# A first message pass that gathers normalized features instead of rows of a precomputed table

## The chip, the cores and the metric

One program runs on one core of a Trainium2 chip. The metric is the device time of one execution in microseconds (us), and the time of a version is the median of its runs. Besides the runs, one execution was recorded by the hardware profiler; all rows shown here are from it. The engines are PE (TensorE: matmul; PEld is its weight load), DVE (VectorE), ACT (ScalarE), POOL (GpSimd) and SP (SyncE, here only an issuer of DMAs).

## The reference, cut to what matters

A graph of 3125 nodes with 128 features and 53125 directed edges, sorted by destination, goes through four layers, each added to the input and normalized:

```python
# layer 0: four dense-looking steps over the same graph
for l in range(4):
    agg = segment_sum(x[src], dst);  h = relu((x + agg) @ W1[l] + b1[l]);  x = h @ W2[l] + b2[l]
# layer 1, 8 kinds of edges: a mean over each kind, the kernel's "first pass"
out = x @ root + bias
for r in range(8):
    s = segment_sum((x @ W[r])[src] * (edge_type_8 == r), dst)
    c = segment_sum(edge_type_8 == r, dst)
    out = out + s / maximum(c, 1)
out = relu(out)
# layer 2, 16 kinds: alpha[kind] * (x @ w_rel[kind])[src] summed at dst, plus indegree * (x @ update), relu
# layer 3, 8 kinds: gate * (x @ W[kind] + bias)[src] summed at dst, plus x @ loop_weight, relu
```

Between the layers stands `y = layernorm(previous input + layer output)`.

## The kernel before, in words

The 3125 nodes are 25 blocks of 128, the edges 416 tiles of 128. The program has these stages.

1. **Setup and adjacency** (0 to 300 us): PE builds the dense adjacency matrix `adj` in SBUF from one-hot products.
2. **Layer 0** (300 to 735 us): four dense multiplications with `adj`, `block_sums` (L1052), first the four early chunks of 512 nodes, then the three late ones; ACT applies the relu (L1330), PE multiplies by the next matrix (`layer_rows`, L987) and DVE adds the bias into `un` (L1683). After the last layer the space of `adj` is reused for everything that follows, so loads and the first norm wait for its last product.
3. **First table** (735 to 806 us): five sets of five blocks are normalized on DVE (`norm`, L1716 to L1736), turned by PE (L1126) and multiplied by the eight kind matrices and the root matrix (L1135). ACT and DVE copy the products out of PSUM (L1357, L1759) and SP writes 512 KB a block to `table1` (L665): row `8 * node + kind` holds `x @ W[kind]`. POOL copies the normalized features into `xn`.
4. **Edge weights** (803 to 866 us, DVE, `edge_weights`): for each edge one over the number of edges of its kind at its destination, `w1`.
5. **Three passes** (806 to 2466 us) of the same form. POOL issues one indirect DMA per tile of 128 edges (`gathers`, L808), which brings 128 rows of 512 bytes into `ring`, a ring of 51 tiles (three turns of 17). ACT scales each tile by its edge weights (`take`, L1384). PE multiplies a one-hot of 128 destinations by the tile (`sums`, L1199) and so adds it to the sum of a block in PSUM; where a tile straddles two blocks it is multiplied twice, so a turn of 17 tiles has 18 steps in three groups of six. DVE makes the one-hots (`hot_group`, L1590), adds and normalizes a finished block (`block_sum`, `block_norm`, L1798 to L1817), PE turns it (`transposed`, L1152) and multiplies it for the next table (`products`, L1165), ACT and DVE copy that out (L1406, L1827), and SP writes it (L691). One turn carries the tiles of about one block. A slot of the ring is handed on to POOL by ACT (`hand_on`, L1367) once the group that used it is done. A pass starts to gather when the table before it is written whole.

Every engine has its own fixed order of work and waits on semaphores; nothing is scheduled at run time. In the second and third pass the loop over turns is the same; the second has 16 kinds, the third gates.

## Time and profile before

| | us |
|---|---|
| median of 3 runs (lowest, highest) | 2472.38 (2465.28, 2472.53) |
| the profiled execution | 2467.42 |
| its span, first to last instruction | 2465.6 |
| POOL busy, indirect gathers x1248 | 1347.4, 1216.7 |
| PE busy, mean granted clock | 1431.8, 0.754 |
| DVE busy | 923.6 |
| ACT busy | 633.1 |

Busy time of a group is summed over the whole span, so an engine can be busy half of the time and still set the end of each stage, and of an indirect gather the profile counts only the part in which POOL works: from one to the next there are 0.30 us more of issue. PE's clock is told as the granted share of full speed: 1.0 is 2.4 GHz and 0.5 is 1.2 GHz, and the number of a stretch is the mean of the two over it.

### The profile page before, as it was taken

Reading aid. Unit: us, or ns where it says so; the run is one execution under the profiler, and the core shown is the slowest. Engines: PE = TensorE matmul, PEld = TensorE weight load, DVE = VectorE, ACT = ScalarE, POOL = GpSimd, SP = SyncE. Lnnn points to the kernel's source line nnn. Section 1 sums busy time; section 2 is a strip of 40 time slices with the busy share of each in tenths; the row PEclk is TensorE's granted clock in tenths of the full one; section 3 lists DMA queues with packets and bytes.
Section 4 is the critical chain, followed back from the end, with each engine's and each line's share of the span. In section 5 each row is a group of like instructions: output and inputs, shape, how many; then the busy total and the mean of one; then the engine's idle time right before and its main releaser. Section 6 shows DMA issues by size and latency. Waiting matters only on the chain.

```text
span 2465.6 us, 30012 instructions
## 1 busy us (share of the span) xinstructions
PE 1431.8 (58%) x6376; PEld 929.6 (38%) x6481; DVE 923.6 (37%) x2317; ACT 633.1 (26%) x1671; POOL 1347.4 (55%) x1541
## 2 busy tenths in 40 slices
PE   5666599999999065555565255555454333333333
PEld 3333355455444044434343143334333233333333
DVE  6999622121116943333222453333333321222221
ACT  0677400000013043333333154444443100000000
POOL 1000015230221777777777477777777477777775
PEclk8888899999999577677766676767766666556665
DMA  0000001000026233333323222222222122222221
GB/s 20 0 0 0 18 14 11 7 5 0 5 40 246 56 89 106 106 105 106 105 87 106 83 69 78 77 78 78 76 70 77 60 55 56 55 55 56 56 55 47
DMA packets 120619, 148.87 MB, mean 60 GB/s; under 512 B 74779, under 2 KB 88737, under 8 KB 117362
## 3 DMA queue, kind: packets, MB, share of 16 engines
q0 software_dynamic: 40000, 81.89, 13.1%
q1 hardware_dynamic: 80562, 66.31, 8.2%
q8 instruction: 25, 0.41, 0.1%
q14 instruction: 32, 0.26, 0.0%
HBM read 91.39 MB, written 56.72 MB: 60 GB/s over the span
## 4 chain that ended last, share of the span: by engine, by line
POOL 45%; PE 26%; issue 17%; DVE 5%; ACT 4%; DMA 1%; SPq 1%; POOLq 1%; ACTq 0%; DVEq 0%
POOL adj L808 45%; PE acc L1052 16%; PE acc L943 4%; ACT adj L1305 2%; PE acc L1135 2%; ACT acc L1309 1%; PE acc L1199 1%; PE misc L987 1%; PE acc L1165 1%; DMA table<-adj 1%; DMA adj<-table,adj 1%; DVE adj L1937 0%; DVE adj L1908 0%; ACT adj L1384 0%; DVE adj L1910 0%
## 5 line engine op out<-in xcount | busy, mean ns | idle before, releaser
L808 POOL DMA_INDIRECT adj<-table,adj x1248 | 1216.7, 975 | 442.4 <-issue 378.4
L1199 PE MATMUL acc<-adj 128*128 x2640 | 524.9, 374 | 702.9 <-ACT adj L1384 321.8
L1199 PEld LDWEIGHTS acc<-adj 128*128 128x128 f32 x2640 | 473.0, 274 | 770.6 <-issue 770.2
L1384 ACT ACTIVATE adj<-adj 128x128 f32<-128x128 f32 x832 | 263.2, 390 | 573.5 <-DMA adj<-table,adj 489.3
L1052 PE MATMUL acc<-adj,feat 128*128 (+2 forms) x2042 | 399.7, 352 | 6.6 <-DVEq L1639 3.5
L758 POOL TENSOR_TENSOR node_rep<-node_rep,compb 128x128 f32<-128x128 f32 x128 | 57.2, 447 | 547.2 <-DMA node_rep<-in_L_gnn_weight_dram 538.4
L1590 DVE TENSOR_TENSOR adj<-acc,drel 128x768 f32<-128x768 f32 (+1 forms) x148 | 139.9, 948 | 453.7 <-PE acc L1199 453.2
L1052 PEld LDWEIGHTS acc<-adj,feat 128*128 (+1 forms) x2100 | 185.6, 98 | 212.0 <-DVEq L1639 3.4
L1165 PE MATMUL acc<-adj 128*128 128x512 f32 (+1 forms) x350 | 197.9, 711 | 71.5 <-ACT adj L1399 71.5
L943 PE MATMUL acc<-feat 128*128 128x400 bf16 x625 | 142.1, 387 | 76.6 <-ACT acc L1309 68.9
L1603 DVE TENSOR_SCALAR feat<-feat 128x400 bf16<-128x400 int16 x625 | 156.4, 318 | 0.0
L1367 ACT ACTIVATE adj<-feat 128x4 int32 (+1 forms) x196 | 33.7, 198 | 447.0 <-PE acc L1199 441.3
L1165 PEld LDWEIGHTS acc<-adj 128*128 128x128 f32 x350 | 83.2, 267 | 159.8 <-ACT adj L1399 84.3
L943 PEld LDWEIGHTS acc<-feat 128*128 128x128 bf16 x625 | 78.2, 126 | 141.0 <-issue 126.8
L1590 DVE TENSOR_TENSOR adj<-node_iob,drel 128x384 f32<-128x384 bf16 (+1 forms) x148 | 75.2, 551 | 147.7 <-PE acc L1199 147.7
L1330 ACT ACTIVATE feat<-acc,l0c 128x512 f32<-128x512 f32 (+1 forms) x28 | 15.6, 635 | 358.2 <-PE acc L1052 292.1
L1305 ACT ACTIVATE adj<-acc 128x800 f32 (+1 forms) x98 | 81.1, 827 | 54.8 <-PE acc L943 54.6
L1309 ACT ACTIVATE acc<-zerob 128x800 f32<-128x800 bf16 x98 | 82.5, 842 | 9.0
L1599 DVE TENSOR_TENSOR feat<-node_rep,temp 128x640 bf16<-128x640 bf16 x125 | 69.1, 553 | 21.4 <-PE acc L943 12.1
L1683 DVE TENSOR_TENSOR temp<-misc,l0c 128x512 f32<-128x512 f32 (+1 forms) x21 | 13.3, 633 | 144.9 <-PE misc L987 144.9
L1827 DVE COPY adj<-acc 128x512 f32<-128x512 f32 x25 | 17.3, 692 | 127.0 <-PE acc L1165 127.0
L1798 DVE TENSOR_TENSOR adj<-acc,adj 128x128 f32<-128x128 f32 x75 | 21.7, 289 | 103.2 <-PE acc L1199 103.0
(266 smaller groups left out, 1070.4 us busy)
## 6 DMA issues: line engine op xcount, KB each, us to landing
table<-adj SPq DMA_DIRECT2D x50, 512.0 KB, 2.8
table<-adj SPq DMA_DIRECT2D x25, 1024.0 KB, 4.2
adj<-table,adj POOLq DMA_INDIRECT x1250, 2.5
table<-adj SPq DMA_DIRECT2D x25, 64.0 KB, 1.8
temp<-in_x_dram SPq DMA_DIRECT2D x6, 256.0 KB, 3.1
out_dram<-adj SPq DMA_DIRECT2D x24, 64.0 KB, 1.6
wrel<-node_rep SPq DMA_DIRECT2D x16, 64.0 KB, 3.0
adj<-in_L_gnn_W_dram SPq DMA_DIRECT2D x2, 512.0 KB, 5.1
```

The costliest lines, as they stand in the source:

```text
L758: nc.gpsimd.tensor_tensor(sl_tmp if b else sl_out, of_b, by, ALU.mult).then_inc(slice_step, 1)
L808: pool.indirect_dma_start(ring[:, p_, 0:D], None, table, bass.IndirectOffsetOnAxis(ap=gidx[:, p_:p_ + 1], axis=0)).then_inc(msgs_in[u.r][c ...
L943: nc.tensor.matmul(acc[:, bass.ds(places[q * FG + j], FCOLS)], flo[:, q, :, j], foh[:, q, j, :], start=False, stop=True, skip_group_check= ...
L1052: last = nc.tensor.matmul(acc[:, c * KB:c * KB + chunk(c)], x3[:, s, bass.ds(b, 1), :].rearrange("p b f -> p (b f)"), adj[:, bass.ds(b, 1) ...
L1165: nc.tensor.matmul(o, xT1[:, b.r, :], table, start=True, stop=True).then_inc(prod_full[j], 1)
L1199: last = nc.tensor.matmul(acc[:, bass.ds(blk[s], width)], hot[:, c, j, :], ring_flat[:, bass.ds(place[s], width)], start=False, stop=True, ...
L1305: nc.scalar.activation(adj[:, :, bass.ds(i * (TURN * 2 * FB) + r * 2 * FB, 2 * FB)].rearrange("p h (k n) -> p h k n", k=2), fslots[r % FSL ...
L1309: nc.scalar.activation(fslots[r % FSLOTS], zerob[:, 0:FCOLS].unsqueeze(1).to_broadcast([P, 2, FCOLS]), ACT.Copy).then_inc(zeroed, 1)
L1384: last = nc.scalar.activation(o, o, ACT.Copy, scale=WEIGHT[ph][:, bass.ds(tiles_from(u, c) + j, 1)])
L1590: return nc.vector.tensor_tensor(o, numbers.unsqueeze(1).to_broadcast([P, n, P]), drel[:, bass.ds(s, n)].unsqueeze(2).to_broadcast([P, n, ...
L1599: nc.vector.tensor_tensor(flo[:, q, :, :], node_iof[:, :, :], flow[:, bass.ds(k * (FG * FNB) + q * FG, FG)].unsqueeze(1).to_broadcast([P, ...
L1603: last = nc.vector.tensor_scalar(foh[:, q, j, :], col_io, fkey[:, bass.ds(k * (FG * FNB) + q * FG + j, 1)], None, ALU.is_equal)
```

## The change

The first pass no longer gathers rows of `x @ W[kind]`. It gathers the normalized features themselves, from `tablex` (1.6 MB instead of 12.8 MB), sums them by destination and kind, and multiplies by the eight matrices after the sum.

- **No first table.** The 25 products with eight matrices, their copies and the 25 writes of 512 KB go. What stays of that stage is the root part: each block is turned by PE, multiplied by the root matrix (128 columns) and the bias is added by a product with a row of ones (`root_rows`); ACT copies the turned block and the result. POOL's copies into `xn` go too: DVE normalizes in place.
- **Loads and norms inside the last layer.** What these need lies in the first eight blocks of `adj`'s space, which are free once PE has multiplied them (`low_free`). PE then does the first four chunks' `layer_rows` between late blocks instead of after them. DVE prepares keys and the walk (`first_walk`, 17 small operations of at most 104x512), finishes the first four chunks of `un` and normalizes 16 blocks in three sets; the last nine blocks are normalized after the layer, and the fourth write of `tablex` follows.
- **One-hots by kind.** A tile now spans at most two fine blocks of 16 destinations. Its key is `128 * (fine block within the tile) + 16 * kind + (destination mod 16)`, and its one-hot has 256 columns. PE uses the gathered tile as the stationary side and multiplies it by the two halves of the one-hot, always both: 34 products of 128 columns a turn instead of 18. The sums of a block are two PSUM banks of 512 columns (4 fine blocks x 8 kinds x 16 nodes). ACT copies one half and DVE the other (`kind_part`) into `agg_t`, turned so that `block_out` can multiply by the eight matrices in eight accumulating products.
- **One-hot slots.** There are three slots again, each now of up to three tiles, so a turn has eight pieces where it had three groups.
- **Order within a turn of the first pass.** PE loads its places in four register loads a turn (one per part of 4, 4, 4 and 5 tiles) where it had two. ACT copies the products for the next table before it scales the first tiles of the next turn.
- **In the second pass** the indegree is read from the sums (129 columns) and multiplied into `rest` there, as the first pass no longer has such a column.
- **Setup.** POOL checks in ten small operations that every tile keeps within two fine blocks and every turn within its block; otherwise the general path is taken.

```diff
+PIECES = ((2, 2), (2, 2), (2, 2), (2, 3))
+NP1, WIDE = 8, 2 * P
+GROUPS1 = 2 * CHUNKS
+SETS = ((0, 5), (5, 5), (10, 6), (16, 9))
+EARLY_SETS, SETW = 3, 9
...
+            def normalized_rows(b, n):
+                sp.wait_ge(xnorm_set, b + n)
+                sp.dma_start(tablex[b * P:(b + n) * P].rearrange("(b p) f -> p b f", p=P), xn[:, b:b + n, :]).then_inc(tablex_set, 16)
...
-                        late(l, 0, BLOCKS - 1)
+                        late(l, 0, LOWB - 1)
+                        block_sums(l, range(4, CH), LOWB - 1, False).then_inc(low_free, 1)
+                        for c in range(4):
+                            layer_rows(l, c)
+                            late(l, LOWB + c, LOWB + c + 1)
+                        late(l, LOWB + 4, 16)
+                        pe.wait_ge(key_ready, 1)
+                        pe.wait_ge(un_ready, made(l, 1))
+                        for c in range(TC):
+                            last = nc.tensor.transpose(misc[:, c * TQ:(c + 1) * TQ], key_b[:, c * P:(c + 1) * P], ident[0:TQ, 0:TQ])
+                        last.then_inc(key_ps, 1)
+                        late(l, 16, BLOCKS - 1)
                     block_sums(l, range(4, CH), BLOCKS - 1, False).then_inc(sum_ready, 1)
-                for c in range(CH):
+                for c in range(4, CH):
+                    if c == 5:
+                        pe.wait_ge(key1_set, 1)
...
+            def block_out(b):
+                pe.wait_ge(agg_ready, b.num(2, 2))
+                after(pe, prod_free[SIDE], blocks_seen(1, b))
+                for r in range(R1):
+                    last = nc.tensor.matmul(acc[:, OUT_AT:OUT_AT + D],
+                                            agg_t[:, b.odd(), r, :, :].rearrange("p f n -> p (f n)"),
+                                            tab1[:, r * D:(r + 1) * D], start=(r == 0), stop=(r == R1 - 1))
+                last.then_inc(out_full, 1)
...
+            def kind_sums(t):
+                for c in range(2 if t.last() else len(SIZES)):
...
+                    pe.wait_ge(tiles_in, t.num(TPT, PARTS_AT[c] + n))
+                    j = 0
+                    for i, n_ in enumerate(PIECES[c]):
+                        k = 2 * c + i
+                        pe.wait_ge(hot_ready, t.num(NP1, k + 1))
+                        for z in range(n_):
+                            for w in range(2):
+                                last = nc.tensor.matmul(acc[:, bass.ds(blk[2 * j + w], P)], ring[:, place_of(t, c) + j, 0:D],
+                                                        hot1[:, hot_slot(t, k), z, w * P:(w + 1) * P],
+                                                        start=False, stop=True, skip_group_check=True)
+                            j += 1
+                        last.then_inc(group_free, 1)
+                    yield c
+            def first_pass():
+                def body(t):
+                    b = t.plus(-1)
+                    for c in kind_sums(t):
+                        if not b.exists():
+                            continue
+                        if c == 1:
+                            if not t.last():
+                                pe.wait_ge(agg_ready, b.num(2, 2))
+                                for h in range(2):
+                                    clear_bank(2 * b.odd() + h)
+                            block_out(b)
+                        elif c == 2:
+                            transposed(1, b)
+                    if b.exists():
+                        if t.last():
+                            transposed(1, b)
+                        products(1, b)
+                for b in range(4):
+                    clear_bank(b)
+                turns_by_six(pe, body)
+                last = At(BLOCKS // 3, 0)
...
+            def first_pass():
+                def body(t):
+                    b, more = t.plus(-1), not t.last()
+                    take(1, t, 1)
+                    after_group(1, t, 0)
+                    if b.exists():
+                        hand_on(1, t.plus(2), 3)
+                        kind_part(b)
+                    if more:
+                        hand_on(1, t.plus(3), 0)
+                        take(1, t, 2)
+                    after_group(1, t, 1)
+                    if more:
+                        hand_on(1, t.plus(3), 1)
+                    if b.exists():
+                        deviation(1, b)
+                    if more:
+                        take(1, t, 3)
+                        after_group(1, t, 2)
+                        hand_on(1, t.plus(3), 2)
+                    if b.exists():
+                        features(1, b)
+                    if b.exists():
+                        table_parts(b)
+                    if more:
+                        take(1, t.plus(1), 0)
+                take(1, At(0, 0), 0)
...
+            def first_walk():
+                dve.wait_ge(low_free, 1)
+                nc.vector.tensor_copy(idx0[:, :], tile8[:, :]).then_inc(counting, 1)
+                dve.wait_ge(counting, 1)
+                nc.vector.tensor_single_scalar(idx0[:, :], idx0[:, :], 3, ALU.arith_shift_right).then_inc(idx0_set, 1)
+                nc.vector.tensor_copy(kind_iob[:, 0:P], node_io[:, :])
...
+                    elif c == 3:
+                        hold(dve, un_ready, made(l, c + 1))
+                        dve.wait_ge(x_in, 32)
+                        for i in range(EARLY_SETS):
+                            norm(i)
+                        if not general:
+                            first_keys()
...
+            def kind_hots(t, c):
+                j = PARTS_AT[c]
+                for i, n_ in enumerate(PIECES[c]):
+                    k = 2 * c + i
+                    at_ = t.num(NP1, k - NB)
+                    if not (isinstance(at_, int) and at_ < 0):
+                        dve.wait_ge(group_free, t.num(NP1, k - NB + 1))
+                    nc.vector.tensor_tensor(
+                        hot1[:, hot_slot(t, k), 0:n_, :], kind_iob.unsqueeze(1).to_broadcast([P, n_, WIDE]),
+                        key1[:, bass.ds(t.num(TPT, j), n_)].unsqueeze(2).to_broadcast([P, n_, WIDE]), ALU.is_equal).then_inc(hot_ready, 1)
+                    j += n_
...
+            def kind_part(b, t, c):
+                dve.wait_ge(group_free, t.num(NP1, 2 * c + 2))
+                nc.vector.tensor_copy(half_kinds(b, 1), half_sums(b, 1)).then_inc(agg_ready, 1)
...
+                def body(t):
+                    b, before = t.plus(-1), t.plus(-2)
+                    kind_hots(t, 0)
+                    if before.exists():
+                        table_parts(1, before)
+                    if b.exists():
+                        kind_part(b, t, 0)
+                    kind_hots(t, 1)
+                    if not t.last():
+                        kind_hots(t, 2)
+                    if b.exists():
+                        block_sum(1, t, b, False)
+                        block_norm(1, b)
+                    if not t.last():
+                        kind_hots(t, 3)
...
+                if ph == 2:
+                    nc.vector.scalar_tensor_tensor(y1[:, :], flat(rest), indeg[:, bass.ds(b.num(), 1)], own, ALU.mult, ALU.add
+                                                   ).then_inc(sum_read, 1)
```

One turn of the first pass on ACT, as its order of instructions shows it where the turns are unrolled. L1384 and L1561 scale gathered tiles, L1367 and L1544 hand slots on, L1394 and L1571 are the square root of a block's norm, L1399 and L1576 copy the turned block, L1406 and L1583 copy products, L1592 copies half of the sums. Before:

```order
L1384 ACTIVATE adj<-adj 128x128 x8
L1367 ACTIVATE adj<-feat 128x5
L1367 ACTIVATE adj<-feat 128x4
L1394 ACTIVATE adj<-adj,epst 128x1
L1384 ACTIVATE adj<-adj 128x128 x5
L1367 ACTIVATE adj<-feat 128x4
L1384 ACTIVATE adj<-adj 128x128 x4
L1399 ACTIVATE adj<-acc 128x128
L1367 ACTIVATE adj<-feat 128x4
L1406 ACTIVATE adj<-acc 128x512 x2
```

And after:

```order
L1544 ACTIVATE adj<-adj 128x5
L1592 ACTIVATE adj<-acc 128x4x8x16
L1544 ACTIVATE adj<-adj 128x4
L1561 ACTIVATE adj<-adj 128x128 x4
L1544 ACTIVATE adj<-adj 128x4
L1571 ACTIVATE adj<-adj,epst 128x1
L1561 ACTIVATE adj<-adj 128x128 x5
L1544 ACTIVATE adj<-adj 128x4
L1576 ACTIVATE adj<-acc 128x128
L1583 ACTIVATE adj<-acc 128x512 x2
L1561 ACTIVATE adj<-adj 128x128 x8
```

The four tiles that open the next turn stood ahead of the turned block and the product copies; now they stand behind both, and so behind PE's products of this turn.

The end of the first pass on PE, after its last sums. L1152 and L1267 turn a block, L1165 and L1285 are the products for the second table, L1292 the eight products of `block_out`, L1256 and L1434 belong to the second pass. Before:

```order
L1152 MATMUL acc<-ident,adj 128x128
L1165 MATMUL acc<-adj 128x512 x3
L1165 MATMUL misc<-adj 128x512
L1165 MATMUL acc<-adj 128x128
L1256 MATMUL misc<-ident,adj 128x16 x2
```

And after:

```order
L1292 MATMUL acc<-adj 128x128 x8
L1267 MATMUL acc<-ident,adj 128x128
L1285 MATMUL acc<-adj 128x128
L1285 MATMUL acc<-adj 128x512 x2
L1285 MATMUL misc<-adj 128x512
L1285 MATMUL acc<-adj 128x512
L1434 MATMUL misc<-ident,adj 128x16 x2
```

This is the last block (24). Ahead of it block 23 has the same rows; before, block 23 was added while the last sums ran. The last two blocks now have eight products each between their sums and their norm.

SP between the last layer and the first gather. Before:

```order
L619 DMA adj<-in_x_dram 128x24x128
L621 DMA adj<-in_x_dram 53x128
L622 DMA adj<-in_L_gnn_W_dram 128x8x128
...
L656 DMA adj<-in_L_gnn_update_dram 128x128
L665 DMA table<-adj 128x1024 x5
```

And after:

```order
L673 DMA temp<-in_dst_dram 1x416x1
L676 DMA adj<-in_dst_dram 96x512
...
L680 DMA adj<-in_x_dram 128x24x128
...
L690 DMA tablex<-adj 128x5x128 x2
L690 DMA tablex<-adj 128x6x128
L699 DMA feat<-in_dst_dram 96x514
...
L690 DMA tablex<-adj 128x9x128
L724 DMA adj<-in_L_gnn_attn_b_dram 128x128
```

Seven loads for keys and walk stand ahead of the features, the first three writes of the table come while the layer still runs, and the fourth stands ahead of the small loads of the later passes.

## Rows read from the trace of the kernel before

**Rows 1.** Busy time of each engine by stretch; "x" counts instructions, PEclk is the granted clock.
```profile
806.00:870.00 64.00, 3.53 (x13) 1.86 (x15) 59.68 (x70) 3.62 (x12) 52.91 (x37) 0.51 0.15 39
870.00:930.00 60.00, 41.42 (x190) 30.94 (x191) 24.43 (x64) 26.32 (x91) 45.97 (x47) 0.81 0.35 108
930.00:1354.00 424.00, 243.07 (x920) 169.07 (x933) 127.25 (x328) 142.87 (x493) 322.45 (x334) 0.70 0.33 102
```

**Rows 2.** Timeline of POOL: start, duration, instruction, [idle before it and its releaser].
```profile
806.11 1.23 POOL L808 DMA_INDIRECT adj<-table,adj  x1 [15.02 <-DMA table<-adj]
809.75 1.93 POOL L808 DMA_INDIRECT adj<-table,adj  x1 [0.30 <-issue]
...
1353.40 0.95 POOL L808 DMA_INDIRECT adj<-table,adj  x1 [0.30 <-issue]
1378.77 0.95 POOL L808 DMA_INDIRECT adj<-table,adj  x1 [24.42 <-DMA table<-adj]
```

**Rows 3.** Timeline, the end of the last layer and the first set of norms.
```profile
694.59 2.42 ACT L1330 ACTIVATE feat<-acc,l0c 128x512 f32<-128x512 f32 x4 [65.53 <-PE acc L1052]
728.95 1.14 PE L987 MATMUL misc<-l0c,feat 128*128 128x128 f32 x8
735.54 0.28 DVE L1683 TENSOR_TENSOR adj<-acc,l0c 64x128 f32<-64x128 f32 x1
739.25 0.83 DVE L1716 TENSOR_TENSOR feat<-adj 128x640 f32<-128x640 f32 x1 [1.86 <-DMA adj<-in_x_dram]
742.46 1.38 DVE L1736 TENSOR_SCALAR feat<-feat,adj 128x128 f32<-128x128 f32 x5
```

**Rows 4.** Groups of POOL's instructions in the third pass: count, busy us, mean ns.
```profile
L808 POOL DMA_INDIRECT adj<-table,adj x416 | 393.5, 946 | 149.8 <-issue 126.5 <-DMA table<-adj 23.3
```

**Rows 5.** Groups over the whole span, kept apart by shape; same columns.
```profile
L1384 ACT ACTIVATE adj<-adj 128x128 f32<-128x128 f32 x832 | 263.2, 390 | 573.5 <-DMA adj<-table,adj 489.3 <-DVE adj L1943 65.2 <-DVEq L1973 18.9
L1590 DVE TENSOR_TENSOR adj<-node_iob,drel 128x384 f32<-128x384 bf16 x144 | 73.7, 554 | 146.9 <-PE acc L1199 146.9
L1590 DVE TENSOR_TENSOR adj<-node_iob,drel 128x256 f32<-128x256 bf16 x4 | 1.6, 428 | 0.8 <-PE acc L1199 0.8
L1406 ACT ACTIVATE adj<-acc 128x512 f32<-128x512 f32 x50 | 29.8, 597 | 60.9 <-PE acc L1165 60.9
L1827 DVE COPY adj<-acc 128x512 f32<-128x512 f32 x25 | 17.3, 692 | 127.0 <-PE acc L1165 127.0
L1937 DVE SCALAR_TENSOR_TENSOR adj<-feat,adj 104x512 f32<-104x512 bf16 x14 | 10.5, 752 | 0.5
```

**Rows 6.** Timeline of PE, the first sums of the first pass.
```profile
869.68 0.58 PE L1199 MATMUL acc<-adj 128*128 x1 [2.25 <-ACT adj L1384]
```

**Rows 7.** Timeline of PE, early turns of the first pass; two instructions make one product.
```profile
886.67 0.33 PE L1152 MATMUL acc<-ident,adj 128*128 128x128 f32 x1 [0.92 <-DVE adj L1816]
887.11 1.60 PE L1199 MATMUL acc<-adj 128*128 x12
888.54 2.75 PE L1165 MATMUL acc<-adj 128*128 128x512 f32 x6
892.42 2.90 PE L1199 MATMUL acc<-adj 128*128 x24
897.10 0.33 PE L1152 MATMUL acc<-ident,adj 128*128 128x128 f32 x1 [1.78 <-DVE adj L1816]
899.45 2.94 PE L1199 MATMUL acc<-adj 128*128 x12 [2.02 <-ACT adj L1384]
```

**Rows 8.** Register loads of PE's queue (L915): ns min/median/max.
```profile
L915 PEldq TENSOR_LOAD <-walk_i x152: 540/1595/2258, 866.0 to 2450.7; - x152
```

**Rows 9.** Timeline, the end of the first pass.
```profile
1360.59 0.28 DVE L1798 TENSOR_TENSOR adj<-acc,adj 128x128 f32<-128x128 f32 x1
1362.59 0.35 DVE L1816 TENSOR_SCALAR adj<-adj 128x128 f32<-128x128 f32 x1
1373.71 0.34 SPq L691 DMA_DIRECT2D table<-adj  x1
```

More of the change, by code:

```diff
@@ L177, in carve @@
             return a
+        hot_at = used[0]
+        hot = carve([P, NB, G, P])
+        un = carve([P, BLOCKS, D])
+        xn = carve([P, BLOCKS, D])
+        tab1 = carve([P, (R1 + 1) * D])
+        rows = carve([P, 3, D])
+        key1 = carve([P, TILES], BF16)
+        kind_iob = carve([P, WIDE], BF16)
+        idx0 = carve([P, TILES], I32)
+        hot1 = big[:, hot_at:hot_at + NB * G * P].rearrange("p (s j k) -> p s j k", s=NB, j=3)
+        dst_l, et_l = (big[0:TQ, hot_at + i * TW:hot_at + (i + 1) * TW].bitcast(I32) for i in range(2))
+        key_a, key_b = (big[0:TQ, hot_at + i * TW:hot_at + (i + 1) * TW] for i in range(2, 4))
+        assert 4 * TW <= NB * G * P and 3 * WIDE <= G * P
+        LOWB = -(-used[0] * 2 // NA)
+        assert LOWB < 10
         SW = R2 * D
@@ L854, in passes @@
                     else:
-                        gathers(ph, table, of_pairs if ph == 2 else None)
+                        gathers(ph, tablex if ph == 1 else table, of_pairs if ph == 2 else None)
             hold(pool, peak_set, 1)
@@ new lines, in root_rows @@
+            def root_rows(b, general):
+                pe.wait_ge(xTb_ready, b + 3)
+                after(pe, root_free, b - 3)
+                o = acc[:, (b % 4) * KB:(b % 4) * KB + D]
+                nc.tensor.matmul(o, xTb[:, b % 4, :], tab1[:, R1 * D:(R1 + 1) * D], start=True, stop=False)
+                nc.tensor.matmul(o, ones[0:1, :], rows[0:1, 0, :], start=False, stop=True).then_inc(root_full, 1)
+                for j in range(2 if general else 0):
+                    after(pe, gprod_free, 2 * b + j - 1)
+                    nc.tensor.matmul(psum_bank((4, 7)[j]), xTb[:, b % 4, :], tab1[:, j * KB:(j + 1) * KB],
+                                     start=True, stop=True).then_inc(gprod_full, 1)
@@ new lines, in first_pass @@
+            def first_pass():
[20 more added lines that the diff above has]
+                last = At(BLOCKS // 3, 0)
+                block_out(last)
+                transposed(1, last)
+                products(1, last)
@@ L1324, in _, with deviations @@
                                      ACT.Copy).then_inc(hT_ready, 1)
+            def deviations(i):
+                n = SETS[i][1]
+                act.wait_ge(bag_ready, i + 1)
+                nc.scalar.activation(std[:, 0:n], bag[:, 0:n, 1], ACT.Sqrt, bias=epst[:, :]).then_inc(std_ready, 1)
             act.wait_ge(bias_in, 32)
```

582 lines of the change are left out of this document (333 added, 249 removed).

## The prediction, made before the changed kernel ran

> **What bounds the kernel now.** I read the busy shares by stretch first, then POOL's own timeline, then PE, ACT and DVE inside a turn, and last the rows around the three places where POOL stands still. From 806 us to the end POOL issues gathers one after another: 381 of them between 870 and 1354 us, 0.95 us each and 0.30 us of issue behind it [rows 1, 2]. The first of the first pass is at 806.11, the last ends at 1354.35, so that pass takes 548.2 us; then POOL waits 24.4 us for the last write of the next table [rows 2]. PE is busy 57% of the pass (243.07 of 424.00) at a mean clock of 0.70, DVE 30%, ACT 34% [rows 1]. So the end is set by when the first gather can start, by 416 gathers a pass, and by the two gaps between passes. Two things of this change act on that: the first gather comes earlier, and the engines behind POOL get more work a turn, which costs nothing until they fall behind it.
>
> **The start of the gathers.** Before: the late sums end at 729.0, the last row of `un` is done at 735.8 [rows 3], the table takes until 806.1. After: the 25 late blocks took from 694.6 to 729.0, 1.37 us each [rows 3]; eight of them free the space at 705.6. Into the 17 that follow PE puts four groups of `layer_rows` (1.14 each, 4.6; before they came behind the sums) and four small transposes (estimated 1.0): sums end at 734.6. The 17 operations of `first_walk` are at most 0.75 us each (the row of 104x512 with two inputs [rows 5]), 13 us, so the first `un` is ready near 720, and PE asks for it after 8 blocks and the 4 groups, at 721.2: no wait, by little. The features are asked for near 710 behind seven loads. They landed about 10 us after the sums' end before [rows 3], so at 720, hidden too. Three sets of norms, 4.6 us each (739.25 to 743.84 [rows 3]), 14 us for 16 blocks and 1 to 2 more for the sixth block of one, end at 736, beside the sums. Then relu of the first late chunk 0.6 (2.42/4), three short groups 2.7, the last bias 0.7: `un` ends at 738.6. Nine blocks by 4.6/5 are 8.3, less fixed waits: 7.6. The write of 0.6 MB and POOL's wake-up: from the issue of a 1 MB write to the gather behind it 5.06 us passed (1373.71 to 1378.77 [rows 2, 9]), I take 4.4. First gather at 750.6, say 751: **55 us earlier**. If every hidden piece is late, up to 10 us less. The turned blocks and roots (25 blocks, about 1.1 us each) run on PE and ACT beside DVE's edge weights, which need PE only 20 us in.
>
> **The pass as POOL sees it.** The edge weights let the first sums start 63.6 us after the first gather (869.68 against 806.11 [rows 2, 6]) and still will: they start behind the last norm. The scans slow POOL in the same place (1.93 us a gather [rows 2]). What is new is longer one-hots from SBUF. A piece of 256 columns took 428 ns, of 384 554 ns [rows 5], so 0.98 ns a column: 680 ns for two tiles, 932 for three. 24 turns x (7 x 0.680 + 0.932) + 4 x 0.680 = 139 us against 144 x 0.554 = 80. In 870 to 1354 a gather took 368.4/381 = 967 ns, in the third pass, whose one-hots read PSUM, 946 [rows 4] (368.4 and 381 are the sums over [rows 1]): 8 us on 80 us of one-hots, 0.10 us per us. 59 us more make 6. The pass at POOL's pace is 554 us.
>
> The Trainium skill (SBUF — State Buffer, "Who interferes with whom") says that a VectorE instruction with two SBUF inputs and a GpSimd one that reads SBUF exclude each other for the whole instruction. By that rule taken whole POOL would lose up to the 59 us; the trace shows a tenth of it, so the gather needs the port only for a part of its time.
>
> **A turn of the engines behind it.** POOL's turn is 17 x 1.25 plus the above, 21.6 us. Whether the others keep that pace I work out at PE's 2.4 GHz (12 instructions in 1.60, 24 in 2.90 us; at 1.2 GHz 12 take 2.94 [rows 7]). A product of 128 columns is two instructions, 0.24; a part of 4 tiles is 8 products, 1.9, of 5 tiles 2.4; a product of 512 columns 0.92 (2.75/3). Along the chain: part 0 1.9; before part 1 a register load of 1.6 [rows 8] or DVE's copy of a half (0.69 as a plain copy [rows 5]) and one-hot, 1.7; part 1 1.9; two clears and `block_out` 0.5 + 1.9; part 2 1.9, beside which DVE adds and normalizes (1360.59 to 1362.94, 2.35 us [rows 9]); a wait and the transpose 0.9; ACT's five tiles and a register load 1.6; part 3 2.4; products 0.25 + 4 x 0.92 = 3.9; then ACT still copies (0.6 [rows 5]) and scales four tiles at 0.32 (1.3 [rows 5]), of which 0.5 is late. Sum 19.1 us, of it PE works 14.8, 77%. The strided copies of halves may cost twice the plain ones, 1 us a turn more; I take the plain value.
>
> How slow may a turn be? PE starts those 63.6 us late and has 24.5 turns until the last tile, which lands about 5 us after POOL's end: (554 + 5 - 63.6)/24.5 = 20.2 us. At 1.2 GHz PE's 14.8 double, of which some 4 were waits that vanish: 30 us. So a tenth of the time at the low level is free, each further tenth costs 1.1 us a turn, 27 us in all. In the rows PE fell after idling 1.78 and 2.02 us around one transpose, and not after 0.92 us [rows 7]. The new turn has idle of 1.7 us at two places, once with a transpose in it, so it falls now and then. I take 20.3 us a turn, 3 us in all.
>
> The Trainium skill (TensorE: Matmul & The Clock Gate, "HAM oscillation — how this bites in real kernels") describes bursts shorter than the wait for their data, each of which starts cold. If that held each turn as in 930 to 1354 (0.70), it would be the second rival below.
>
> **The gap behind the first pass.** Before 24.4. After, counted from the last gather's end: its tile lands at +2, ACT is through with the product copies of the turn before and both last parts at +4.1, PE with its products, the two parts and DVE's half between them at +8.6; then `block_out` of block 23 1.9, its norm 2.35, transpose and copy 0.8, products with side 3.9, to +17.6; DVE's copies of two quarters and the side 0.8 more, then `block_out` of block 24 1.9 (its output shares a bank with the side), norm 2.35, transpose and copy 0.8, products 3.9, copy 0.7: +28; write and wake-up 5.06: 33. **9 us lost.** Bounds: 29 if copies overlap better, 41 at the low clock.
>
> **Costed at nothing.** POOL's ten checks stand before its wait for DVE in the setup (L737); at 0.75 us each [rows 5] they would cost 8 without that cover. The second pass's indegree adds a copy and a wait of 0.2 us a turn off POOL's path. Second and third pass stay.
>
> **Sum.** -55 + 6 + 9 + 3 = -37 us on the profiled 2467.4: 2430. The median of the runs is 2472.4, 5 above the profiled one; I leave the forecast at 2430.
>
> **The rivals.**
> 1. *The turn decides, mildly.* Turns of 20.8 to 21.8 us, because PE is at the low level for 15 to 25% or the strided copies double: 15 to 39 us more. For it: 0.81 in the first 60 us with PE 69% busy [rows 1]; against: the idle pieces are shorter. 2455.
> 2. *Slower than before: the turn decides at the low clock.* PE's gaps of 1.7 us drop it in nearly every turn, a turn takes 19.1 + 0.4 x 11 = 23.5 us, the pass 63.6 + 24.5 x 23.5 = 639, 80 more: 2507. It decides from 21.8 us a turn, where all is lost. For it: 0.70 in steady state; against: those gaps were waits for gathers that had not landed, and a late PE has none.
> 3. *One-hots lock POOL out* for their whole length: 53 more, 2483.
> 4. *The start is late*: lists, features or norms in the layer miss their cover, PE stops before its key transposes; gathers from 765: 2444.
> 5. *General path*: a check fires. The keys of this graph stay inside, so under 1 in 100.
>
> **Chances.** Forecast (2416 to 2442, its own range) 0.55; rival 1 0.24; rival 4 0.06; rival 2 0.11; rival 3 0.03; rest 0.01. Range 2416 to 2470: it leaves out rival 2 and 3 and a little below. Under 0.3% (7 us) nothing can be told from no change. Faster 0.83, same 0.04, slower 0.13.
>
> **What would show it.** First gather near 751 with three of four `tablex` writes before 740; POOL's gathers unbroken at 1.25 us behind the scans, without waits for ACT's `hand_on`; PE's clock above 0.8 in the first 200 us of the pass; a gap of 33 us before the second pass; later passes of 530 and 520 us. Wrong it is if POOL waits for ACT in the first pass (rivals 1, 2), if one-hots stretch gathers above 1 us on average (3), or if PE stands still before the key transposes (4).

## The result, and the profile after

The changed kernel takes 2477.15 us (median of 9 runs, 2473.07 to 2483.65) where the kernel before takes 2468.74 beside it (9 runs): ratio 1.0033, 95% interval 1.0022 to 1.0044. It is slower by a third of a per cent, and the forecast was 2430 with a range up to 2470. The profiled execution took 2473.07 us, its span is 2471.3.

Read POOL's timeline first, as before: start, duration, instruction, and in brackets the idle time ahead of it with what ended it.

```profile
749.83 1.63 POOL L897 DMA_INDIRECT adj<-tablex,adj  x1 [15.09 <-DMA tablex<-adj]
...
1325.47 0.95 POOL L897 DMA_INDIRECT adj<-tablex,adj  x1 [0.30 <-issue]
1379.22 0.95 POOL L897 DMA_INDIRECT adj<-table,adj  x1 [52.80 <-DMA table<-adj]
...
1935.71 0.95 POOL L897 DMA_INDIRECT adj<-table,adj  x1 [24.45 <-DMA table<-adj]
```

The first gather is 56.3 us earlier (806.11 to 749.83). The first pass then takes 576.6 us instead of 548.2, and the gap behind it 52.8 instead of 24.4 [rows 2]: 28.4 us lost in each. The rest (second pass 532.0 for 530.4, its gap 24.45 for 23.3, third pass 522.4 for 520.1) adds 5. Together -56.3 + 28.4 + 28.4 + 5 = +5.7, which is the difference of the spans.

The groups of POOL's gathers in the first pass, first of the kernel before, then of the changed kernel, and with the latter the one-hots of the first pass, which answer to those of [rows 5]. Columns: count, busy us, mean ns, idle.

```profile
L808 POOL DMA_INDIRECT adj<-table,adj x416 | 421.7, 1014 | 141.6 <-issue 126.0 <-DMA table<-adj 15.0 <-ACT adj L1367 0.6
```
```profile
L897 POOL DMA_INDIRECT adj<-tablex,adj x416 | 450.1, 1082 | 141.6 <-issue 124.6
L2014 DVE TENSOR_TENSOR adj<-adj 128x512 f32<-128x512 bf16 x196 | 133.2, 719 | 71.1 <-PE acc L1312 70.9
```

POOL is not idle longer (141.6 us in both); its gathers are longer, 450.1 us in all against 421.7, and that is the whole first loss. In the third pass, where no one-hot has both inputs in SBUF, a gather takes 952 ns:

```profile
L897 POOL DMA_INDIRECT adj<-table,adj x416 | 395.9, 952 | 150.9 <-issue 126.5 <-DMA table<-adj 24.5
```

Two timelines of one place, POOL and DVE, show how one gather comes to 3 us:

```profile
1136.02 0.95 POOL L897 DMA_INDIRECT adj<-tablex,adj  x1 [0.30 <-issue]
1137.28 3.01 POOL L897 DMA_INDIRECT adj<-tablex,adj  x1 [0.30 <-issue]
1140.59 0.95 POOL L897 DMA_INDIRECT adj<-tablex,adj  x1 [0.30 <-issue]
```
```profile
1137.05 0.34 DVE L2102 TENSOR_SCALAR adj<-adj 128x128 f32 x1
1137.31 2.15 DVE L2014 TENSOR_TENSOR adj<-adj 128x512 f32<-128x512 bf16 x3
1140.84 0.69 DVE L2014 TENSOR_TENSOR adj<-adj 128x512 f32<-128x512 bf16 x1 [1.38 <-PE acc L1312]
```

The gather starts with a run of three one-hots and ends 0.8 us after the run. Two gathers beside a single one-hot show what decides, POOL above and DVE below:

```profile
1286.12 1.43 POOL L897 DMA_INDIRECT adj<-tablex,adj  x1 [0.31 <-issue]
...
1297.95 0.95 POOL L897 DMA_INDIRECT adj<-tablex,adj  x1 [0.30 <-issue]
```
```profile
1286.03 0.69 DVE L2014 TENSOR_TENSOR adj<-adj 128x512 f32<-128x512 bf16 x1 [1.69 <-PE acc L1312]
...
1297.99 0.69 DVE L2014 TENSOR_TENSOR adj<-adj 128x512 f32<-128x512 bf16 x1 [2.42 <-PE acc L1312]
```

The gather that starts 0.09 us into a one-hot is longer and ends 0.83 us after it; the one that starts 0.04 us ahead of a one-hot takes 0.95 us as if alone. From 870 to 1320 us, 71 of 331 gathers start while a one-hot stands, 1.41 us each on average; the other 260 take 0.95 to 0.98 us, but for the one of 3.01 us above, which starts 0.03 us ahead.

The second loss is the gap, and behind it the turn. PE's timeline over one even and one odd turn of the first pass (first tiles of each at 1081.09 and 1101.86):

```profile
1084.60 2.05 PE L1312 MATMUL acc<-adj 128*128 128x128 f32 x16 [1.46 <-DVE adj L2014]
...
1093.38 3.42 PE L1312 MATMUL acc<-adj 128*128 128x128 f32 x20 [1.35 <-DVE adj L2014]
...
1101.86 2.05 PE L1312 MATMUL acc<-adj 128*128 128x128 f32 x16 [0.68 <-ACT adj L1561]
1107.12 2.66 PE L1312 MATMUL acc<-adj 128*128 128x128 f32 x16 [3.21 <-DVE adj L2014]
...
1118.76 4.04 PE L1312 MATMUL acc<-adj 128*128 128x128 f32 x20 [2.65 <-DVE adj L2014]
```

The waits are put down to DVE's one-hots. But the register loads of PE's queue say something else. Loads of the whole pass, then of the even turn and of the odd one (min/median/max in ns):

```profile
L1301 PEldq TENSOR_LOAD <-temp x84: 587/1586/3867, 861.2 to 1325.0; - x84
```
```profile
L1301 PEldq TENSOR_LOAD <-temp x4: 591/628/1244, 1079.7 to 1091.8; - x4
```
```profile
L1301 PEldq TENSOR_LOAD <-temp x4: 1934/2248/3866, 1099.6 to 1115.9; - x4
```

The same four loads, the same loop body, and about three times the length in every second turn. The turns alternate with them: from the first load of a turn to that of the next, 19.84 and 25.28 us at this place, and so throughout from 870 us on: 18.7 to 20.3 in even turns, 23.4 to 26.8 in odd ones. While a load stands, PE is idle for about 1 us in an even turn and about 5.5 in an odd one. That is most of the difference, but not all: PE is also busy longer with the same products. Busy times of the even and of the odd turn shown above, columns as in [rows 1], the last three granted clock, DMA share and GB/s:

```profile
1079.70:1099.60 19.90, 15.68 (x96) 12.78 (x96) 9.36 (x19) 7.25 (x27) 15.46 (x15) 0.91 0.34 107
1099.60:1124.80 25.20, 17.48 (x97) 14.52 (x97) 9.40 (x19) 7.61 (x27) 19.41 (x20) 0.86 0.31 94
```

Of the 5.3 us between them 3.5 are idle time of PE and 1.8 are slower products at the lower granted clock, behind PE's longer stops. What tells odd from even is the address: a turn's row of `walk1` is 17 tiles of two numbers, 136 bytes, so every second row starts 8 bytes off a multiple of 16. The loads of the kernel before read rows of 176 bytes, 11 times 16.

A third thing, in all kernels built on the changed one, adds to the second loss: the sums start late. They start at 823.3 us, 73.5 behind the first gather, where the kernel before had 63.6. Inside the edge weights DVE waits for a product of PE's; the kernel before, then the changed one, then PE's stretch ahead of it:

```profile
827.08 0.58 DVE L1919 COPY adj<-misc 8x416 f32<-8x416 f32 x1 [0.89 <-PE misc L1240]
```
```profile
782.72 0.58 DVE L2203 COPY adj<-misc 8x416 f32<-8x416 f32 x1 [14.73 <-PE misc L1419]
```
```profile
742.70:781.40 38.70, 38.69 (x123) 27.40 (x123) 24.84 (x49) 13.16 (x48) 25.77 (x20) 0.50 0.47 125
```

PE is busy with the turned blocks and roots for these 38.7 us, at the low level throughout, 1.55 us a block.

### The profile page after: what moved, and what is told of

Same layout as the page of the kernel before. It is cut to its first block, busy times and chain, and to the rows that moved or that the text cites. A ratio compares the mean times of both kernels' runs of the same rounds, so it can differ in the third digit from the quotient of the medians.

```text
span 2471.3 us, 32295 instructions
## 1 busy us (share of the span) xinstructions
PE 1534.4 (62%) x7521; PEld 1062.6 (43%) x7644; DVE 984.1 (40%) x2355; ACT 635.8 (26%) x1695; POOL 1381.2 (56%) x1530
## 4 chain that ended last, share of the span: by engine, by line
PE 36%; POOL 32%; issue 15%; DVE 10%; ACT 4%; DMA 1%; DVEq 1%; POOLq 0%; ACTq 0%; SPq 0%
POOL adj L897 32%; PE acc L1150 15%; PE acc L1312 8%; PE acc L1039 4%; PE acc L1285 2%; DVE adj L2014 2%; PE acc L1292 2%; ACT adj L1487 2%; ACT acc L1491 1%; ACT adj L1561 1%; PE misc L1083 1%; PE acc L1237 1%; PE acc L1261 0%; PE acc L1236 0%; DVE feat L1818 0%
## 5 line engine op out<-in xcount | busy, mean ns | idle before, releaser
L897 POOL DMA_INDIRECT adj<-table,adj x832 | 799.2, 961 | 330.2 <-issue 252.0
L1378 PE MATMUL acc<-adj 128*128 x1760 | 367.8, 387 | 538.7 <-DMA adj<-table,adj 281.1
L1378 PEld LDWEIGHTS acc<-adj 128*128 128x128 f32 x1760 | 330.2, 286 | 591.9 <-issue 591.9
L897 POOL DMA_INDIRECT adj<-tablex,adj x416 | 450.1, 1082 | 141.6 <-issue 124.6
L1561 ACT ACTIVATE adj<-adj 128x128 f32<-128x128 f32 x832 | 260.4, 388 | 316.6 <-DMA adj<-table,adj 256.0
L1312 PE MATMUL acc<-adj 128*128 128x128 f32 x1664 | 253.8, 317 | 107.1 <-DVE adj L2014 96.6
L1312 PEld LDWEIGHTS acc<-adj 128*128 128x128 f32 x1664 | 236.2, 227 | 136.1 <-issue 136.0
L1285 PE MATMUL acc<-adj 128*128 128x512 f32 (+1 forms) x350 | 170.2, 627 | 35.9 <-ACT adj L1576 35.9
L2014 DVE TENSOR_TENSOR adj<-adj 128x512 f32<-128x512 bf16 x196 | 133.2, 719 | 71.1 <-PE acc L1312 70.9
L1544 ACT ACTIVATE adj<-feat 128x4 int32 (+1 forms) x98 | 17.6, 203 | 428.1 <-PE acc L1378 428.1
L1285 PEld LDWEIGHTS acc<-adj 128*128 128x128 f32 x350 | 72.1, 249 | 90.3 <-issue 47.0
L2083 DVE TENSOR_TENSOR adj<-acc,adj 128x128 f32<-128x128 f32 x50 | 14.6, 292 | 176.5 <-PE acc L1378 100.0
```

Of the source, the lines that this page charges most:

```text
L897: pool.indirect_dma_start(ring[:, p_, 0:D], None, table, bass.IndirectOffsetOnAxis(ap=gidx[:, p_:p_ + 1], axis=0)).then_inc(msgs_in[u.r][c ...
L1285: nc.tensor.matmul(o, xT1[:, b.r, :], table, start=True, stop=True).then_inc(prod_full[j], 1)
L1312: last = nc.tensor.matmul(acc[:, bass.ds(blk[2 * j + w], P)], ring[:, place_of(t, c) + j, 0:D], hot1[:, hot_slot(t, k), z, w * P:(w + 1) * P],
L1378: last = nc.tensor.matmul(acc[:, bass.ds(blk[s], width)], hot[:, c, j, :], ring_flat[:, bass.ds(place[s], width)], start=False, stop=True, ...
L1561: last = nc.scalar.activation(o, o, ACT.Copy, scale=WEIGHT[ph][:, bass.ds(tiles_from(u, c) + j, 1)])
L2014: nc.vector.tensor_tensor(hot1[:, hot_slot(t, k), 0:n_, :], kind_iob.unsqueeze(1).to_broadcast([P, n_, WIDE]), key1[:, bass.ds(t.num(TPT, ...
```

## The experiments

Theory A: loads off 16 bytes slow the odd turns, the turns of PE, ACT and DVE set the end of the pass, and POOL's longer gathers lie hidden under it. Each edit is to the changed kernel unless said otherwise. Ratios are to the kernel before on the same chip: 2472.55 us beside e1, e1b, e2 and e3, 2468.73 beside f2, f5, f7 and f8.

**e1: rows of 144 bytes.** A row gets room for one tile more.

```diff
+WTPT = TPT + 1
-        walk1 = temp[0:1, 0:2 * TILES].bitcast(I32)...
+        walk1 = temp[0:1, 0:2 * WTPT * TURNS].bitcast(I32)...
-    walk1[0:1, bass.ds(t.num(TPT, PARTS_AT[c]), n), :]
+    walk1[0:1, bass.ds(t.num(WTPT, PARTS_AT[c]), n), :]
```

> The rows that PE's register loads read (L1301) get a stride of 144 bytes in place of 136, so that each load starts at a multiple of 16 bytes; nothing else moves. Theory A (in the changed kernel the loads of 32 bytes take 0.6 us in even turns and 1.94 in odd ones because every second row starts 8 bytes off 16, and PE stands 2.8 + 2.3 us a turn in them): all loads of 8 numbers take 0.6 us (up to 1.0 beside one-hots), the odd turns fall from 25.0 us to the even ones' 20.0, the gap behind the first pass from 52.8 to 31-37 us, and the time by 16-22 us, to 2451-2457. POOL's pass stays near 577. Rival B (PE waits for one-hots, whose three slots come free too late, and the loads only stand beside that wait): the odd turns stay at 24-25 us, and the time at 2471. Rival C (a load's time goes by which copy of the loop body it is in, not by its address): loads stay at 0.6 and 1.94.

Measured: 2450.0 us (5 runs), ratio 0.9908 (0.9895 to 0.9922). The loads of the pass, and the gap:

```profile
L1302 PEldq TENSOR_LOAD <-temp x88: 587/594/1217, 861.0 to 1325.2; - x88
```
```profile
1355.11 0.95 POOL L898 DMA_INDIRECT adj<-table,adj  x1 [31.15 <-DMA table<-adj]
```

Odd and even turns are now alike, 18.6 to 20.3 us until 1031; from there on the gathers pace them, at 20.6 to 24.2. The gap fell by 21.6 us, POOL's pass from 577 to 570, the span of the profiled execution by 21.8 and the median by 27, just beyond the band. The changed kernel ran on another chip; by the ratios the gain is 1.25%, 31 us. Rivals B and C fall: neither the one-hots nor the loop body changed. The page's row of the sums (L1312, L1313) puts 96.6 us of PE's idle time down to one-hots in the changed kernel and 50.0 in e1: about half of that wait was loads.

**e1b: the same, every row 8 bytes off.** The table starts two numbers later (`temp[0:1, 2:2 + ...]`).

> The same stride of 144 bytes, and the whole table 8 bytes further on, so that every load starts 8 bytes off a multiple of 16. Theory A: loads of 8 numbers take 1.94 us in every turn, every turn takes about 25 us, the consumers need 24.4 x 25 = 610 us from 812, so the second pass starts near 1430 in place of 1379, POOL waits for them, and the time is 2510-2535. Rivals B and C: as the changed kernel, 2471-2477.

Measured: 2540.82 us, 1.0279 (1.0263 to 1.0295), even slower than expected.

```profile
L1302 PEldq TENSOR_LOAD <-temp x75: 1931/2426/3990, 857.3 to 1322.7; - x75
```
```profile
1439.70 0.95 POOL L898 DMA_INDIRECT adj<-table,adj  x1 [85.75 <-DMA table<-adj]
```

From 870 us on all turns are 23.6 to 26.6 us. So the address alone is worth 91 us between e1 and e1b, with the same number of bytes and instructions. POOL now stands for ACT as well (47 us), since its ring is full.

**e2: kind numbers in PSUM**, rows of 136 bytes. A bank is freed by letting the four products share two.

```diff
-        PRODUCT_BANKS = {1: (5, 6, 7, 5), 2: (4, 5)}
+        PRODUCT_BANKS = {1: (5, 6, 5, 6), 2: (4, 5)}
+        kind_ps = misc[:, 0:WIDE]
-    hot1[...], kind_iob.unsqueeze(1).to_broadcast([P, n_, WIDE]),
+    hot1[...], kind_ps.unsqueeze(1).to_broadcast([P, n_, WIDE]),
```

> The one-hots of the first pass take the 256 kind numbers from a PSUM bank in place of SBUF; to free the bank, the four products share two banks, which may cost PE up to 1 us a turn. Rows as the changed kernel's (136 bytes). Theory A (the turn of PE, ACT and DVE sets the pass; POOL's longer gathers are one-hots that hold it, up to 2 us where three stand in a row, and hidden): behind the first 35 gathers none takes over 1.0 us, the mean falls from 1.082 to about 0.99, POOL's pass from 577 to 541-552, the gap grows by as much, and the time stays within 10 us of the changed kernel, 2461-2481. Rival D (POOL's longer gathers set the pass): the time falls with them, by 25-35 us, to 2436-2446. Rival E (one-hots do not hold POOL; the longer gathers come from elsewhere): gathers stay at 1.08.

Measured: 2483.03 us, 1.0049 (1.0032 to 1.0065), 2 us above the band. POOL's group and the one-hots' group:

```profile
L897 POOL DMA_INDIRECT adj<-tablex,adj x416 | 413.1, 993 | 152.9 <-issue 119.8
L2012 DVE TENSOR_TENSOR adj<-misc,adj 128x512 f32<-128x512 f32 x196 | 132.4, 716 | 70.4 <-PE acc L1312 69.9
```

The one-hots take as long as before (the groups mix pieces of two and three tiles; kept apart, 683 and 687 ns for 128x512, 946 and 951 for 128x768), and the gathers are free of them: behind the first 39, which stand beside the scans and the rest of the edge weights, none takes over 1.05 us. POOL's pass falls from 577 to 551 us (of the 37 us won in gathers it waits 18 for ACT to hand slots on), the gap grows to 81.7, the time does not fall. POOL's longer gathers were real and hidden; rivals D and E fall.

**f2: two banks alone**, to price the bank.

> The changed kernel with its four products in two PSUM banks (5, 6, 5, 6) and nothing else, to price the bank that the PSUM numbers took. Theory A: a turn grows by up to 1 us and sets the pass, so 2477 becomes 2480-2500; with the PSUM numbers alone it was 2483, so that run's loss against 2477 is the bank's. Rival: two banks cost nothing, 2477.

Measured: 2485.88 us, 1.0071 (1.0053 to 1.0089); gap 63.1 us.

```profile
L897 POOL DMA_INDIRECT adj<-tablex,adj x416 | 448.5, 1078 | 141.6 <-issue 123.5
```

The bank costs 0.4% against the changed kernel, clear of both intervals. That it is also what kept e2 from gaining fits, but e2's interval (1.0032 to 1.0065) overlaps both its neighbours'. Between f2 and e2 POOL won 35.4 us of gather time with little of it in the total. The price of the one-hots is 35.4 us on 133 us of them, 0.27 us per us.

**e3: both, rows of 144 bytes and PSUM.**

> Both: rows of 144 bytes and the kind numbers in PSUM. Theory A: turns of 20-21 us, POOL at 1.25-1.26 us a gather: its first pass takes 541-552 us, the gap behind it 30-38, the second pass starts at 1322-1340 and the time is 2415-2433, below both kernels. Rival B: turns stay near 22.5, time 2465-2480. Rival D: 2436-2446, as the PSUM numbers alone.

Measured: 2421.89 us (5 runs), ratio 0.9794 (0.9780 to 0.9807).

```profile
L898 POOL DMA_INDIRECT adj<-tablex,adj x416 | 414.2, 996 | 141.3 <-issue 125.0
```
```profile
1329.57 0.95 POOL L898 DMA_INDIRECT adj<-table,adj  x1 [33.66 <-DMA table<-adj]
```

It beats both kernels, by 2.1% the kernel before. Beside e1 on the same chip POOL's gathers fell by 29.4 us and the time by 28.1: with the slow turns out of the way nearly every microsecond that the one-hots take from POOL counts.

**e4, e5, e7, e8: four kernels on a chip where all were slower.** e4 is the changed kernel with two register loads a turn, of 16 and 18 numbers (the second ahead of the second quarter), e5 the same on e3. e7 is e3 with DVE's order changed:

```diff
                     kind_hots(t, 0)
-                    if before.exists():
-                        table_parts(1, before)
+                    kind_hots(t, 1)
                     if b.exists():
                         kind_part(b, t, 0)
-                    kind_hots(t, 1)
+                    if before.exists():
+                        table_parts(1, before)
```

e8 is the kernel before with `WROW = 2 * SPT + 10`, rows of 184 bytes.

> The changed kernel with its rows of 136 bytes, and two register loads a turn (16 and 18 numbers, the second behind the first quarter's products with the one-hots) in place of four. Theory A' (what costs is where a load stands: the load of the last quarter stands behind the transpose of the normalised block, so nothing covers it): PE's 0.7-1.0 us (even turns) and 2.1-2.3 us (odd) before the last quarter go, the slow first load stays slow; a turn falls by 1 to 1.6 us on average from 22.6, the gap from 52.8 to 33-42, the time to 2451-2467 where the changed kernel has 2477. Rival F (a load off 16 bytes costs by its numbers, so that two loads of 16 and 18 stand as long as four of 8 and 10): odd turns stay at 25, the time at 2470-2485.

> Rows of 144 bytes, kind numbers in PSUM, and two loads a turn. Theory A (with turns of 20.2 us below POOL's 21.4 the gathers set the pass): POOL's pass stays at 541, only the tail gains from the shorter turns: gap 31-34 in place of 33.7, time 2417-2423, within 5 us of the kernel with four loads (2422). Rival G (PE's turn still sets the pass even there): 0.7-1.0 us a turn less are 17-24 us, 2398-2405.

> Rows of 144 bytes, kind numbers in PSUM, and DVE makes the second quarter's one-hots before it copies the finished sums and the finished products, in place of behind them. Theory A: POOL sets the pass, so the order changes only the tail: 2416-2426. Rival B (the wait for one-hots holds PE): turns of 20.2 fall below 19, but with POOL at 21.4 a turn the time moves by under 5 us too, so only the turns behind the start (the first ten, in which the consumers catch up) can show it.

> The kernel before, whose walk rows have 176 bytes (11 times 16), with rows of 184 bytes, so that every second row starts 8 bytes off a multiple of 16; two loads a turn of 18 to 21 numbers. Theory A: in odd turns these loads take about three times as long (1.6 us to 4-5 us), in even turns 1.6 as before; PE stands up to 7 us more in an odd turn, most of it beside its waits for weights (158 us in the first pass), so the time grows by 0 to 50 us: 2472-2520. Rival C (the address does not matter): loads of 1.6 us in all turns and 2472.

Measured: 2851.92, 2847.43, 2798.2 and 2771.5 us, where the kernel before took 2750.66 beside them. All times lie outside what was expected. In these traces ACT and DVE wait for up to 33 us where no record ends the wait. The costliest such wait of e8, whose code is the kernel before's but for the stride (us, times, longest):

```profile
ACT adj L1367 <- remote: 963.2, 70, 32.0
```

What held them is open, and so these times say nothing of the theories. e5, e7 and e8 were run again on another chip, as f5, f7 and f8; e4 was not, so its two theories stay untested. The lengths of the loads can still be read: in e4 loads of 16 numbers took 1.11 us at a multiple of 16 bytes and 3.8 to 4.7 off it.

**f5: e5 again.**

> The same kernel as e5 (rows of 144 bytes, kind numbers in PSUM, two loads a turn), beside a run of the kernel before at its usual 2470 us, if this chip gives it. By the traces of e4 and e5 the second load, of 18 numbers behind the first quarter, takes 3.2 us, 2.2 of them with PE idle, where the four loads of 8 to 10 numbers stand 0.7-1.0 us a turn in all: so a turn is 1.2-1.5 us longer, 21.5 us, beside POOL's 21.4. Theory A (the consumers' turn sets the time as soon as it is above POOL's pace): gap of 40-50 us in place of 33.7, time 2428-2440. Rival F (only the number of loads matters): 2417-2423.

Measured: 2446.67 us, 0.9923 (0.9901 to 0.9944), slower than the band: two loads cost 25 us against four (e3, on another chip; 1.3% by the ratios, 17 us between the spans).

```profile
L1302 PEldq TENSOR_LOAD <-temp x43: 1108/1129/3505, 872.7 to 1313.8; - x43
```
```profile
1348.95 0.95 POOL L898 DMA_INDIRECT adj<-table,adj  x1 [56.13 <-DMA table<-adj]
```

The second load takes 3.3 to 3.5 us, though it starts at a multiple of 16, and PE stands 2.1 to 2.5 in it. POOL's pass is unchanged (539.6 us). Rival F falls: what counts is what a load waits and what covers it, not the number of loads.

**f7: e7 again.**

> The same kernel as e7 (rows of 144 bytes, kind numbers in PSUM, the second quarter's one-hots ahead of the two copies). Theory A: POOL sets the pass, the time is 2416-2426 as with the order unchanged (2422). Rival B (PE's wait for one-hots costs): the waits of PE behind one-hots, 54 us in the first pass of e3, fall by half or more, and if they set anything the time falls by 10 us or more, to 2412 or less.

Measured: 2423.06 us, 0.9820 (0.9804 to 0.9837), as e3. PE's waits for one-hots between 870 and 1290 us, in e3 and in f7:

```profile
PE acc L1313 <- DVE adj L2021: 52.9, 38, 1.6
```
```profile
PE acc L1313 <- ACT adj L1562: 55.9, 24, 4.5
...
PE acc L1313 <- DVE adj L2021: 7.0, 6, 1.3
```

They go, turns shorten to 16.6 to 18.9 us in the first 130 us, and from 995 on PE waits instead for ACT's weighted tiles, that is for gathers. Nothing is won, as theory A had it: POOL sets this pass.

**f8: e8 again.**

> The same kernel as e8 (the kernel before, its walk rows moved from 176 to 184 bytes). By e8's trace the two loads of an odd turn take 5.0 and 6.1 us in place of 1.6 and 1.6. Theory A: PE, which waits 158 us for weights in the first pass, takes these 8 us an odd turn mostly out of its waits: +0 to +30 us, 2470-2500, with the loads of odd turns at 5.0 and 6.1. If the loads are 1.6 here, the slow loads were that chip's.

Measured: 2470.27 us (10 runs), 1.0007 (0.9997 to 1.0017).

```profile
L915 PEldq TENSOR_LOAD <-walk_i x152: 532/1637/6193, 871.6 to 2454.2; - x152
```

In [rows 8] the longest was 2258. In the first pass the loads of odd turns take 5.0 and 6.0 us here, in the kernel before's own code, and cost nothing that can be told from noise, since PE waits for gathers there anyway. The same fault is free where gathers set the pace and costs 22 to 31 us where PE's turn does (the changed kernel against e1).

## Why the prediction was wrong

- **The start: right.** 749.83 us for 751. Last row of `un` at 738.0 (738.6), the last norm to 745.2, the scans from 749.3.
- **The turn: the step that failed.** The sum of 19.1 us, 20.3 with the clock, took a register load at 1.6 us from [rows 8] at two places, one of them beside DVE's copy, and let the other two loads be covered. The even turns come out as it says, 19.8 us on average. In the odd ones loads take 1.93 to 3.87 us, PE is idle for 2.8 and 2.3 us in the two that were priced and for 0.5 in the others, its products then run slower, and a turn takes 25.1. The threshold was worked out at 20.2, the mean was 22.5, and that is above the break-even of 21.8 which rival 2 named. e1 and e1b show the cause. Rivals 1 and 2 had the place and the size between them (20.8 to 21.8, and 23.5 us), both with the clock at the root. It was not the root, as aligning the loads alone undoes the loss, but it carried a part: over all odd turns PE is busy 17.9 us at a granted clock of 0.85, over the even ones 15.9 us at 0.92, so about 2 of the 5.3 us. The mean over the pass hides it. Busy times from 870 to 1320 us as in [rows 1], the last three columns granted clock, DMA share and GB/s, of the changed kernel and of e1:

```profile
870.00:1320.00 450.00, 338.27 (x1922) 277.18 (x1941) 187.31 (x380) 153.98 (x520) 349.13 (x332) 0.88 0.32 99
```
```profile
870.00:1320.00 450.00, 342.82 (x2013) 278.43 (x2033) 196.77 (x399) 163.38 (x546) 347.25 (x338) 0.91 0.33 102
```

  PE was at the high level for over three quarters of the time in both (0.88 is 76% at 2.4 GHz, 0.91 is 82%). A load had been priced by the loads of another table, without asking what its own address was. The sign named for rivals 1 and 2, POOL waiting for ACT in the first pass, hardly showed (1.8 us): the turns' lag went into the gap.
- **The start of the sums: a term taken over unchanged, and 10 us off.** The sums were to start 63.6 us behind the first gather, because the roots (1.1 us a block) would be done when DVE needs PE. They took 1.55 us a block at the low level, DVE waited 14.7 us, and the sums started 73.5 us behind. Where the turn sets the pass, as in the changed kernel, this should be up to 10 us of the gap; no run undid it, so its price is not shown.
- **The gap: right but for the turn.** 33 forecast, 52.8 measured; 31.2 and 33.7 once the loads are aligned (e1, e3). The 20 us between are the lag that PE, ACT and DVE gathered in the odd turns.
- **One-hots against POOL: mis-sized.** 0.10 us per us, 6 us more in the pass, was taken from a mean over the kernel before, whose one-hots of 0.55 us stand in pairs of 1.0 us. Measured 0.27 per us (f2, e2): the pass went from 548.2 to 576.6. Rival 3 had it at full length, 53. The cost is not in proportion: a gather that starts while one-hots stand is held to their end, or to the end of one of them, so longer stretches catch more gathers and hold each for longer. In the kernel before (870 to 1354 us) 54 gathers are caught and held 0.17 us each, in the changed one (870 to 1320) 71, and 0.46 us each. In the changed kernel it hides beneath the turn; with the loads aligned it costs 28 us (e1 to e3). The Trainium skill (SBUF — State Buffer, "Who interferes with whom") has a VectorE instruction with two SBUF inputs contend with a GpSimd one that reads SBUF, and one with a single SBUF input, outside the two-port modes, not at all. The runs agree with the second half (e2). Of the first they show 27% of the one-hots' time on average, and in one direction only: a gather that starts second waits, a one-hot that starts beside a running gather takes its 0.69 us. I had weighed the page against a mean and dropped it.
- **Later passes: nearly.** 532.0 and 522.4 for 530 and 520. A gather takes 952 ns in the third pass where [rows 4] has 946; 951 to 954 in all kernels built on the changed one, 944 in f8. It is 4 us in all, and its cause is open.
- **The sum.** Forecast: -55 for the start, +6 for the one-hots, +9 for the gap, +3 for the turn. Measured: -56 for the start, +28 in the pass for the one-hots, +28 in the gap, which holds the turn's share too, and +5 in the later passes, for which nothing was forecast. With aligned loads alone the time is 2450 (e1), inside the range; with the second price gone too, 2422 (e3).

## What to carry to other kernels

When an engine reads numbers into registers inside a loop, give its rows a stride and a start that are multiples of 16 bytes, and look at the shortest, median and longest load: a mean, or a wait that is put down to the neighbour, hides it. A turn that differs between even and odd iterations of one body points to an address. Before pricing a conflict by the mean over a pass, look at which instruction starts first and how long the other stretches without a break: one-hots with both inputs in SBUF took 27% of their time from gathers, the same work with an input in PSUM none, and that was worth 28 us as soon as POOL set the pace, and next to nothing before. A term that is said to stay as it was needs its own look too, when another engine gets new work ahead of it.

## What the hardware showed that was not expected

- A register load of 8 numbers takes 0.59 us at a multiple of 16 bytes and 1.93 us 8 bytes off; of 10 numbers 1.08 and 2.43. Rows of 144 bytes start 16 bytes off a multiple of 32 in every second turn and are fast in all (e1). Other offsets were not tried.
- Some loads take about twice that at one place of the loop, behind the first quarter's products: 3.2 to 3.9 us for 8 numbers off 16 bytes (changed kernel, e1b, and e2 too, so not the one-hots' SBUF input), 3.3 to 3.5 for 18 aligned numbers (f5) where [rows 8] has 1.6. Its cause is open.
- A gather is lengthened by a one-hot with both inputs in SBUF only where it starts while the one-hot stands: 71 such gathers took 1.41 us on average, the others 0.95 to 0.98 but for one.
- A one-hot of 128x512 takes the same with the numbers in PSUM (683 ns) as in SBUF (687).
- PE stayed at the low level (granted clock 0.50) for 38.7 us in which it was busy without a break.
- On one chip all kernels, the one before too, ran 11 to 16% slower, and the four traces from there have waits that no record ends.
